# Last steps of the attention part in their own order, softplus moved to the first pairs, twelve residual tiles loaded in one go

## The chip, the cores and the metric

The kernel runs on one core of one Trainium2 chip. The metric is the device time of one execution in microseconds (us); the value compared is the median over several executions. The engines are called as the profile calls them: PE is TensorE, PEld its weight loads, DVE VectorE, ACT ScalarE, POOL GpSimd, and SP the engine that issues nearly all DMAs.

## What is computed

Two transformer layers on 32 sequences of 192 tokens (64 image patches and 128 text tokens), width 256, all in float32. `_layernorm` is the usual normalisation over the last axis.

```python
h = _L0_tok_ref(x, L0_tok_W, L0_tok_b)                       # patches @ W + b
h = concatenate([h, take(weight, x_txt)], axis=1)            # text embeddings
h = h + _L0_attn_ref(_layernorm(h), wq, wk, wv)              # causal softmax attention, one head
h = h + _L0_ffn_ref(_layernorm(h), w_up, w_down)             # ternary weights, rms-normed, gelu, 256-1024-256
h = h + _L1_attn_ref(_layernorm(h), omega, Win, Wl, bl, Wv, bv, Wout)   # a recurrence over the 192 steps
h = h + _L1_ffn_ref(_layernorm(h), routing, experts)         # 8 experts on the first 2 x 256 rows
...
# in _L1_attn_ref:
xi, z = split(x @ Win.T)
log_lam = -8 * softplus(omega) * sigmoid(xi @ Wl.T + bl); lam = exp(log_lam)
v = xi @ Wv.T + bv
h_t = lam_t * (h_prev - 2 v_t (v_t . h_prev) / (v_t . v_t)) + (1 - lam_t) * xi_t
out = (silu(z) * h) @ Wout.T
```

## The kernel before

The program has three parts, each a block that all five engines enter and leave together.

**Part A** (`part_a`, about 0 to 449 us) is the first layer. Work is done in 16 pairs of sequences; a pair is three tiles of 128 tokens. Matrix products are split into a "hi" and a "lo" half (`_hi` made by a copy, `_lo` by a subtraction), which are multiplied separately. The order is written by hand in one list, `order`, that all engines walk: `run` calls `step(g)` for g = -4 to 15, and in a step every entry of the list is done for pair g + offset. The offset is 0 for the feed-forward entries (`up`, `gelu`, `add`, `down`, `ss`, `rscale`, `h2`), 1 for the middle of attention (`pT`, `v`, `pv`, `h1`, `root2`, `scale2`, `x2T`, `x2_split`, `exp_table`) and 2 to 4 for what comes earlier. So in step 14 there is nothing left to do for offsets 2 and up, and in step 15 only pair 15's feed-forward is left. Steps 2 to 11 are a hardware loop. `prepare(g)` holds what is done once, ahead of a step.

The entries that matter here, for pair n:
- `up` k = 0 to 7: PE multiplies by the ternary up weights; `gelu` k: ACT computes gelu, DVE (k 0 to 4) or ACT (5 to 7) makes `gelu_hi`, POOL makes `gelu_lo`; `add` k: DVE adds the squares. In pair 15 alone DVE makes `gelu_lo` for k = 1, 3, 5, 7.
- `down` k = 0, 1, 2: PE multiplies by the down weights; `down.0` waits for each `gelu_lo` in turn. `ss`: PE sums the squares, DVE writes `rms_mean`; `rscale`: POOL's `rms_root`, then DVE's `rms_scale`; `h2`: DVE's final `residual` (L688), which SP stores to DRAM (L285, L287). `up.0` and `up.1` of the next pair wait for it, for they use its PSUM banks.
- `h1`: DVE's `residual` of attention with the statistics of the second norm (L651 to L662); `root2`: POOL's `ln_roots` (L366); `scale2`: DVE's `x_normed` (L681); `x2T`: PE transposes it; `x2_split`: ACT and DVE make `x2T_hi` and `x2T_lo`.
- `turn_win` and `fold` prepare weights of part B: `turn_win` transposes raw_Win on PE (8 instructions, L791), ACT copies it to `Win_rows` (L423), and eight `fold` products of 512 columns (L799) multiply it with raw_Wl. They stand in step 15: `turn_win` and `fold.0` first, one fold after `up.4`, six behind `down.2`.
- The softplus of omega (L494 to L523): `softplus_arg` ahead of step 14, ACT's Exp and Ln at `exp_table` of step 14 with three loads of function tables (L428 to L432), `softplus_one` in `scale2` of pair 15, `softplus_rest` (nine small DVE instructions) ahead of step 15. SP then writes the result to DRAM (L254), and part B reads it as `channel_rows`.

**Part B** (`part_b`, to about 891 us) is the recurrence, in 48 tiles of four time steps, 128 rows of 256 each. SP loads `B_residual` tiles (`load`, L986), 128 KB each, into 12 buffers: four ahead of the loop over i, then tile i + 9 in round i, so that tiles 4 to 7 come in the rounds -5 to -2 and tiles 8 to 11 in the rounds -1 to 2, each just ahead of that round's `B_scan_in` transfer. That transfer (L1033) is four DMAs of 256 KB, 1 MB a round, from one buffer in SBUF to another with the layout that the recurrence needs. ACT may write the staging buffer again (L1206) only when the transfer of two tiles before has landed, and DVE's step of the recurrence (L1241) and POOL's `B_decayed_u` (L1084) wait for it as well. PE alternates between projections (L1350) and the small product of each time step (L1362).

**Part C** is the expert layer and is not touched.

## Time and profile before

| | us |
|---|---|
| median of 3 runs | 974.67 (972.14 to 975.5) |
| the profiled execution's own time | 972.92 |
| its span in the profile | 970.9 |
| PE busy | 933.2 (96%) |
| DVE busy | 791.1 (81%) |
| ACT busy | 591.7 (61%) |
| POOL busy | 544.8 (56%) |

The span is what the rows below lie in; the execution's own time is 2.0 us longer. A busy share says how long instructions of an engine were under way, not that the engine did useful work at its peak. The granted clock of PE is given as a share of full speed: 1.00 is 2.4 GHz and 0.50 is 1.2 GHz.

### The profile page before, as it was taken

Reading aid. Unit: us, or ns where it says so; the run is one execution under the profiler, and the core shown is the slowest. Engines: PE = TensorE matmul, PEld = TensorE weight load, DVE = VectorE, ACT = ScalarE, POOL = GpSimd, SP = SyncE. Lnnn points to the kernel's source line nnn. Section 1 sums busy time; section 2 is a strip of 40 time slices with the busy share of each in tenths; the row PEclk is TensorE's granted clock in tenths of the full one; section 3 lists DMA queues with packets and bytes.
Section 4 is the critical chain, followed back from the end, with each engine's and each line's share of the span. In section 5 each row is a group of like instructions: output and inputs, shape, how many; then the busy total and the mean of one; then the engine's idle time right before and its main releaser. Section 6 shows DMA issues by size and latency. Waiting matters only on the chain. (4 is left out here: it accounts for less than half of the span.)

```text
span 970.9 us, 19833 instructions
## 1 busy us (share of the span) xinstructions
PE 933.2 (96%) x6016; PEld 835.8 (86%) x6016; DVE 791.1 (81%) x2380; ACT 591.7 (61%) x1180; POOL 544.8 (56%) x674
## 2 busy tenths in 40 slices
PE   7899999999999999988999999999999999998998
PEld 6799999999999999865688888888888888887887
DVE  4887777778877777774589999999999988996787
ACT  2266666666666666674667667667667766753442
POOL 4267666666666666444455455445455556552673
PEclk9999999999999999999999999999999999999999
DMA  6001111111111132003899999999999999994220
GB/s 227 24 29 44 39 45 44 43 43 43 43 43 43 43 106 80 17 17 114 109 140 154 153 156 162 146 157 159 158 156 170 180 167 150 148 147 84 99 65 23
DMA packets 63020, 96.35 MB, mean 99 GB/s; under 512 B 12372, under 2 KB 32988, under 8 KB 62300
## 3 DMA queue, kind: packets, MB, share of 16 engines
q1 hardware_dynamic: 61396, 91.19, 50.6%
q0 software_dynamic: 1536, 4.20, 1.4%
q8 instruction: 37, 0.61, 0.3%
q14 instruction: 43, 0.35, 0.2%
q10 hardware_dynamic: 8, 0.00, 0.0%
HBM read 31.90 MB, written 13.11 MB: 46 GB/s over the span
## 5 line engine op out<-in xcount | busy, mean ns | idle before, releaser
L341 POOL TENSOR_TENSOR gelu_lo<-gelu_out,gelu_hi 128x384 fp32r<-128x384 f32 x124 | 146.0, 1206 | 29.0 <-DVE gelu_hi L559 28.5
L1072 POOL TENSOR_TENSOR B_y<-B_scan_in,B_states 128x512 f32<-128x512 f32 x47 | 60.6, 1290 | 79.3 <-ACT B_states L1161 79.3
L765 PE MATMUL psAB<-ternary_down,gelu_hi 128*128 128x256 f32 x384 | 97.0, 291 | 5.8 <-POOL gelu_lo L341 4.9
L698 PE MATMUL psAB<-x2T_hi,ternary_up 128*128 128x384 f32 x256 | 92.7, 362 | 0.8 <-DVE residual L688 0.6
L765 PE MATMUL psAB<-ternary_down,gelu_lo 128*128 128x256 f32 x384 | 93.4, 282 | 0.0
L698 PE MATMUL psAB<-x2T_lo,ternary_up 128*128 128x384 f32 x256 | 86.2, 337 | 0.0
L1350 PE MATMUL psAB<-Win_hi,B_x_hi 128*128 128x512 f32 x192 | 83.4, 434 | 0.0
L765 PEld LDWEIGHTS psAB<-ternary_down,gelu_hi 128*128 128x128 f32 x384 | 72.2, 188 | 10.4 <-POOL gelu_lo L341 8.8
L1084 POOL TENSOR_TENSOR B_decayed_u<-B_scan_in 128x512 f32<-128x512 f32 x48 | 62.2, 1295 | 29.1 <-DMA B_scan_in<-B_stage 24.1
L1257 DVE SCALAR_TENSOR_TENSOR psAB<-B_decayed_u,psAB 128x128 f32<-128x128 f32 x192 | 68.0, 354 | 12.5 <-PE psAB L1362 11.3
L1362 PEld LDWEIGHTS psAB<-B_partial_dots,B_minus_same_batch 128*128 128x128 f32 x384 | 65.3, 190 | 14.3 <-DVE B_partial_dots L1241 4.2
L1350 PE MATMUL psAB<-Win_hi,B_x_lo 128*128 128x512 f32 x192 | 75.5, 393 | 0.0
L1350 PE MATMUL psAB<-Win_lo,B_x_hi 128*128 128x512 f32 x192 | 75.3, 392 | 0.0
L765 PEld LDWEIGHTS psAB<-ternary_down,gelu_lo 128*128 128x128 f32 x384 | 72.6, 189 | 0.0
L1078 POOL TENSOR_TENSOR B_v_scale<-B_half_vv,half_powers 128x1 f32<-128x1 f32 x48 | 26.4, 551 | 78.8 <-ACT B_v_squared L1182 75.7
L410 ACT ACTIVATE gelu_out<-psAB 128x384 f32<-128x384 f32 x128 | 62.6, 490 | 10.3 <-PE psAB L698 10.0
L1241 DVE CUSTOM_DVE_ANT_0 B_products<-B_scan_in,psAB 128x128 f32<-128x128 f32 x192 | 55.1, 287 | 13.4 <-DVE psAB L1257 8.0
L1246 DVE TENSOR_TENSOR psAB<-psAB,B_scan_in 128x128 f32<-128x128 f32 x192 | 57.5, 299 | 6.5
L578 DVE TENSOR_TENSOR gelu_sq_sum<-gelu_sq_sum,gelu_sq 128x384 f32<-128x384 f32 x105 | 61.1, 582 | 1.7
L1362 PE MATMUL psAB<-B_partial_dots,B_minus_same_batch 128*128 128x1 f32 x384 | 54.7, 212 | 3.9 <-DVE B_partial_dots L1241 3.6
L397 ACT ACTIVATE gelu_sq<-gelu_out 128x384 f32<-128x384 f32 x112 | 57.3, 527 | 0.0
L698 PEld LDWEIGHTS psAB<-x2T_hi,ternary_up 128*128 128x128 f32 x256 | 48.0, 188 | 10.6 <-ACT gelu_out L410 8.0
(275 smaller groups left out, 3318.1 us busy)
## 6 DMA issues: line engine op xcount, KB each, us to landing
B_scan_in<-B_stage SPq DMA_DIRECT2D x192, 256.0 KB, 7.0
patches<-in_patches SPq DMA_DIRECT2D x16, 384.0 KB
B_residual<-layer_out SPq DMA_DIRECT2D x48, 128.0 KB, 4.0
out_dram<-B_residual SPq DMA_DIRECT2D x48, 128.0 KB, 3.6
layer_out<-residual SPq DMA_DIRECT2D x32, 128.0 KB, 1.8
raw_Win<-in_experts SPq DMA_DIRECT2D x3, 768.0 KB, 4.3
raw_Wl<-in_experts SPq DMA_DIRECT2D x3, 768.0 KB, 4.2
layer_out<-residual SPq DMA_DIRECT2D x32, 64.0 KB, 1.9
```

The costliest lines, as they stand in the source:

```text
L341: nc.gpsimd.tensor_tensor(act_l[:, k, :], act[:, k % DEEP, :], act_h[:, k, :].bitcast(F32), ALU.subtract).then_inc(s["ffn_lo"], 1)
L397: nc.scalar.activation(out, act[:, k % DEEP, :], ACT.Square).then_inc(s["sq_done"], 1)
L410: nc.scalar.activation(act[:, k % DEEP, :], ps[:, 6 + k % 2, 0:GT], ACT.Gelu).then_inc(s["gelu_done"], 1)
L578: nc.vector.tensor_tensor(sqsum[:], sqsum[:], sq[:, k % DEEP, :], ALU.add).then_inc(s["sqsum_done"], 1)
L698: last = nc.tensor.matmul(out, a, b, start=(n == 0), stop=(n == len(terms) - 1))
L765: last = nc.tensor.matmul(ps[:, 6 + k // 2, (k % 2) * D:(k % 2 + 1) * D], x[:, c, k * P:(k + 1) * P], dn_w[:, c, :], start=(c == 0 and x i ...
L1072: nc.gpsimd.tensor_tensor(y[:, j % 2], ring[:, j % R_RING, :, GATE, :], hs[:, j % 2], ALU.mult).then_inc(s["y"], 1)
L1084: nc.gpsimd.tensor_tensor(lu[:, j % 2], ring[:, j % R_RING, :, LAM, :], ring[:, j % R_RING, :, U, :], ALU.mult).then_inc(s["lu"], 1)
L1246: nc.vector.tensor_tensor(state(j, k), state(j, k), ring[:, j % R_RING, k, DRIVE, :], ALU.subtract).then_inc(s["scan"], 1)
L1257: nc.vector.scalar_tensor_tensor(out=state(i, k), in0=lu[:, i % 2, k, :], scalar=dot[:, t % 2:t % 2 + 1], in1=state(i, k), op0=ALU.mult, o ...
L1350: last = nc.tensor.matmul(out, a, b, start=(not biased and ks[0] == 0 and n == 0), stop=(ks[-1] == DC - 1 and n == len(terms) - 1), skip_g ...
L1362: nc.tensor.matmul(dot[:, t % 2:t % 2 + 1], minus[:], part[:, t % 2:t % 2 + 1], start=True, stop=True).then_inc(s["dot"], 1)
```

## The change

Four things are changed.

1. Step 14 gets an order of its own, `order_late`: `h1` stands behind `gelu.4`, `root2` behind `h1`, `scale2` behind `exp_table`, `x2_split` behind `x2T` and `turn_win` (now with offset 1) behind `x2_split`. In step 15 the folds 0 to 3 stand first, fold 4 behind `up.4` and folds 5 to 7 behind `down.2`. From pair 14 on DVE makes `gelu_lo` for odd k and adds squares with the two-input form that it had for pair 15 alone.
2. Softplus is computed in the first pairs: the vectors are loaded ahead of step -2, `softplus_arg` follows `x_split` of pair 0, Exp and `softplus_one` follow `pT_split` of pair 0, Ln follows `t_split` of pair 1 (with a table load before it and one after, back to Exp), and `softplus_rest` stands ahead of step 12. At `exp_table` of pair 15 nothing is done any more.
3. SP writes `channel_rows` ahead of step 14 instead of step 15.
4. In part B all 12 `B_residual` tiles are loaded ahead of the loop, each with a semaphore of its own (four are cleared first).

```diff
+        order_late = [w for w in order if w[0] not in ("h1", "root2", "scale2", "x2_split")]
+        for what, behind in (("h1", ("gelu", 4)), ("root2", ("h1", 0)), ("scale2", ("exp_table", 0)), ("x2_split", ("x2T", 0)),
+                             ("turn_win", ("x2_split", 0))):
+            order_late.insert(order_late.index(behind) + 1, (what, 0))
...
-        order_last.insert(0, ("turn_win", 0))
-        for m, behind in enumerate((("turn_win", 0), ("up", 4), ("down", 2), ("down", 2), ("down", 2), ("down", 2), ("down", 2), ("down", 2))):
...
+        order_last = [("fold", m) for m in range(4)] + order_last
+        order_last[order_last.index(("up", 4)) + 1:order_last.index(("up", 4)) + 1] = [("fold", 4)]
+        order_last[order_last.index(("down", 2)) + 1:order_last.index(("down", 2)) + 1] = [("fold", m) for m in (5, 6, 7)]
...
-                step(g, g % 2, g // 2, order_last if g == G - 1 else order)
+                step(g, g % 2, g // 2, order_last if g == G - 1 else order_late if g == G - 2 else order)
...
-                if kind == "gelu" and k in lo_pool and not (isinstance(n, int) and n == G - 1 and k in last_lo_vector):
+                if kind == "gelu" and k in lo_pool and not (late(n) and k in late_lo_vector):
...
+                if kind == "pT_split" and isinstance(n, int) and n == 0:
+                    sc.wait_ge(s["c1"], 1)
+                    nc.scalar.activation(soft[:, 1, :], soft[:, 0, :], ACT.Exp, scale=-1.0).then_inc(s["c2"], 1)
+                if kind == "t_split" and isinstance(n, int) and n == 1:
+                    sc.wait_ge(s["c3"], 1)
+                    nc.scalar.activation(soft[:, 3, :], soft[:, 2, :], ACT.Ln).then_inc(s["c4"], 1)
+                    nc.scalar.activation(warm_back[:], ones[:, 0:1], ACT.Exp)
...
-                if g == G - 2:
-                    softplus_arg()
-                if g == G - 1:
+                if g == G - 4:
                     softplus_rest()
...
+            for q in range(8, R_RES):
+                sp.sem_clear(res_in[q])
             for j in range(2):
                 load(j)
...
-            for j in range(2, 4):
+            for j in range(2, R_RES):
                 load(j)
...
-                if has(i + 9):
+                if has(i + 9) and i + 9 >= R_RES:
                     load(i + 9)
```

How the order of instructions moves is best seen in three places. The rows name line, operation, output and inputs; the line numbers of the change are 4 to 9 higher than those of before.

The first is POOL in steps 14 and 15. Before, all eight `gelu_lo` of pair 14 stand ahead of `root2` (L362 to L366):

```order
L341 TENSOR_TENSOR gelu_lo<-gelu_out,gelu_hi 128x384 x8
L362 TENSOR_SCALAR ln_pair<-ln_moments 128x3
L363 TENSOR_SCALAR ln_pair<-ln_moments 128x3
L366 TENSOR_TENSOR ln_roots<-ln_pair,half_powers 128x6
L358 TENSOR_TENSOR rms_root<-rms_mean,half_powers 128x3
L341 TENSOR_TENSOR gelu_lo<-gelu_out,gelu_hi 128x384 x4
```

Now it is:

```order
L350 TENSOR_TENSOR gelu_lo<-gelu_out,gelu_hi 128x384 x3
L371 TENSOR_SCALAR ln_pair<-ln_moments 128x3
L372 TENSOR_SCALAR ln_pair<-ln_moments 128x3
L375 TENSOR_TENSOR ln_roots<-ln_pair,half_powers 128x6
L350 TENSOR_TENSOR gelu_lo<-gelu_out,gelu_hi 128x384
L367 TENSOR_TENSOR rms_root<-rms_mean,half_powers 128x3
```

Four of the eight `gelu_lo` went to DVE; of POOL's own four (k = 0, 2, 4, 6) the last now stands behind the square roots.

The second is PE from `x2T` of pair 15 to `up.0` of pair 15, at the seam of steps 14 and 15. Before, with the end of `down.2` in the first two rows:

```order
L765 MATMUL psAB<-ternary_down,gelu_hi 128x256
L765 MATMUL psAB<-ternary_down,gelu_lo 128x256
L774 MATMUL psAB<-ones,gelu_sq_sum 128x1 x3
L791 MATMUL psAB<-ident,raw_Win 128x128 x8
L799 MATMUL psAB<-raw_Wl,Win_rows 128x512
L698 MATMUL psAB<-x2T_hi,ternary_up 128x384
```

Now, from the last products of `down.1` over `x2T` and `turn_win` to the first of the 16 products of `down.2`:

```order
L771 MATMUL psAB<-ternary_down,gelu_hi 128x256
L771 MATMUL psAB<-ternary_down,gelu_lo 128x256
L715 MATMUL psAB<-ident,x_normed 128x128 x6
L797 MATMUL psAB<-ident,raw_Win 128x128 x8
L771 MATMUL psAB<-ternary_down,gelu_hi 128x256
```

And from the last of those 16 to `up.0`:

```order
L771 MATMUL psAB<-ternary_down,gelu_hi 128x256
L771 MATMUL psAB<-ternary_down,gelu_lo 128x256
L780 MATMUL psAB<-ones,gelu_sq_sum 128x1 x3
L805 MATMUL psAB<-raw_Wl,Win_rows 128x512 x4
L704 MATMUL psAB<-x2T_hi,ternary_up 128x384
```

The transposes went ahead of `down.2`, and four folds instead of one stand between `ss` and `up.0`.

The third is SP at the start of part B. Before (`ISA x37` are semaphores being cleared):

```order
L986 DMA B_residual<-layer_out 128x1x256 x2
L996 ISA x37
L986 DMA B_residual<-layer_out 128x1x256 x4
L1033 DMA B_scan_in<-B_stage 32x4x512 x4
L986 DMA B_residual<-layer_out 128x1x256
L1033 DMA B_scan_in<-B_stage 32x4x512 x4
```

Now, from the load of raw_Wout on:

```order
L1001 DMA B_raw_Wout<-in_WoutT 128x1024
L993 DMA B_residual<-layer_out 128x1x256 x10
L1005 ISA x37
L1042 DMA B_scan_in<-B_stage 32x4x512 x16
L1032 DMA out_dram<-B_residual 32x4x256
```

The first four `B_scan_in` transfers have no tile load between them any more. On DVE, `softplus_rest` now stands between the loop's last instruction and the first CAST of step 12 (L553); there was nothing there before.

## Rows read from the trace of the kernel before

**Rows 1.** Stages of 25 us; columns: core length, busy (count) of each engine, clock, DMA.

```profile
300.00:325.00 25.00, 24.73 (x185) 23.94 (x184) 19.63 (x56) 16.33 (x34) 17.36 (x17) 1.00 0.14 42
```

**Rows 2.** PE's waits, 401 to 449 us: total, times, longest.

```profile
PE psAB L765 <- POOL gelu_lo L341: 1.9, 3, 1.0
PE psAB L709 <- DVE x_normed L681: 1.3, 1, 1.3
PE psAB L841 <- DVE x2T_lo L551: 1.2, 1, 1.2
PE psAB L799 <- ACT Win_rows L423: 0.7, 1, 0.7
```

**Rows 3.** PE, 414 to 449 us: start, duration, what, idle before it and releaser.

```profile
417.96 0.39 PE L765 MATMUL psAB<-ternary_down,gelu_hi 128*128 128x256 f32 x1 [0.95 <-POOL gelu_lo L341]
421.62 0.88 PE L709 MATMUL psAB<-ident,x_normed 128*128 128x128 f32 x6 [1.26 <-DVE x_normed L681]
424.25 0.73 PE L774 MATMUL psAB<-ones,gelu_sq_sum 128*128 128x1 f32 x6
427.55 0.44 PE L698 MATMUL psAB<-x2T_hi,ternary_up 128*128 128x384 f32 x1
443.23 5.31 PE L799 MATMUL psAB<-raw_Wl,Win_rows 128*128 128x512 f32 x12
```

**Rows 4.** DVE and POOL in steps 14 and 15, columns as in rows 3.

```profile
410.43 1.18 DVE L559 CAST gelu_hi<-gelu_out 128x384 fp32r<-128x384 f32 x1
416.03 0.31 DVE L662 BATCH_NORM_AGGREGATE ln_moments<-ln_stats 128x2 f32<-128x6 f32 x3
430.92 0.56 DVE L565 SCALAR_TENSOR_TENSOR gelu_lo<-gelu_out,gelu_hi 128x384 fp32r<-128x384 f32 x1
418.71 1.35 POOL L366 TENSOR_TENSOR ln_roots<-ln_pair,half_powers 128x6 f32<-128x6 f32 x1
```

**Rows 5.** SP's queue, 427 to 460 us: waits, total, times, longest.

```profile
SPq L292 <- DMA layer_out<-residual: 1.4, 1, 1.4
SPq L73 <- PEq L73: 0.5, 1, 0.5
```

**Rows 6.** Step 12, 350 to 370 us: DVE, POOL and PE.

```profile
358.65 0.96 DVE L551 TENSOR_TENSOR v_lo<-psAB,v_hi 128x768 fp32r<-128x768 f32 x1 [0.61 <-ACT v_hi L386]
361.22 5.53 POOL L341 TENSOR_TENSOR gelu_lo<-gelu_out,gelu_hi 128x384 fp32r<-128x384 f32 x4 [1.15 <-DVE gelu_hi L559]
368.74 0.39 PE L765 MATMUL psAB<-ternary_down,gelu_hi 128*128 128x256 f32 x1 [0.26 <-POOL gelu_lo L341]
```

**Rows 7.** DVE, softplus_rest ahead of step 15: its first instruction and the next after it.

```profile
427.81 0.16 DVE L508 TENSOR_SCALAR softplus<-softplus 128x4 f32<-128x4 f32 x1
429.22 0.36 DVE L559 CAST gelu_hi<-gelu_out 128x384 fp32r<-128x384 f32 x1
```

**Rows 8.** ACT: after t_split of pair 1, and a table load of step 14.

```profile
49.23 0.81 ACT L464 ACTIVATE x2T_hi<-psAB 128x768 fp32r<-128x768 f32 x1 [5.51 <-PE psAB L709]
418.37 1.28 ACT L430 ACT_TABLE_LOAD   x1
```

**Rows 9.** Landing of the first scan transfer, then of residual tile 8: time from issue.

```profile
L1033 SPq DMA_DIRECT2D B_scan_in<-B_stage x4: 605/608/658, 465.8 to 467.8; - x4
DMA to landing us min/median/max: 4.3/6.4/8.2
L986 SPq DMA_DIRECT2D B_residual<-layer_out x1: 623/623/623, 468.4 to 468.4; - x1
DMA to landing us min/median/max: 8.3/8.3/8.3
```

**Rows 10.** ACT and PE at the second scan transfer's landing.

```profile
485.37 0.69 ACT L1206 ACTIVATE B_stage<-psAB,B_v_scale 128x512 f32<-128x512 f32 x1 [2.59 <-DMA B_scan_in<-B_stage]
487.21 0.47 PE L1350 MATMUL psAB<-Wl_Win_hi,B_x_hi 128*128 128x512 f32 x1 [1.11 <-ACT psAB L1143]
```

**Rows 11.** PE's clock, 488 to 491 us; columns as in rows 1.

```profile
488.00:491.00 3.00, 3.00 (x9) 0.50 1.05 137
```

More of the change, by code:

```diff
@@ L112, in part_a @@
         sq = sb("gelu_sq", [P, DEEP, GT])
-        warm, warm_gelu = sb("exp_table_warm", [P, 1]), sb("gelu_table_warm", [P, 1])
+        warm, warm_gelu, warm_back = sb("exp_table_warm", [P, 1]), sb("gelu_table_warm", [P, 1]), sb("exp_table_back", [P, 1])
         sqsum = sb("gelu_sq_sum", [P, GT])
@@ L218, in part_a, with late @@
         lo_pool = [k for k in range(FC) if k not in lo_vector]
-        last_lo_vector = (1, 3, 5, 7)
+        LATE = G - 2
+        late_lo_vector = (1, 3, 5, 7)
+        def late(n):
+            return isinstance(n, int) and n >= LATE
         def wait_lo(eng, n, k):
@@ L227, in wait_lo @@
                 return
-            if isinstance(n, int) and n == G - 1:
-                if k in last_lo_vector:
-                    eng.wait_ge(s["ffn_lo_v"], last_lo_vector.index(k) + 1)
+            if late(n):
+                if k in late_lo_vector:
+                    eng.wait_ge(s["ffn_lo_v"], 4 * (n - LATE) + late_lo_vector.index(k) + 1)
                 else:
-                    eng.wait_ge(s["ffn_lo"], FC * n + k // 2 + 1)
+                    eng.wait_ge(s["ffn_lo"], FC * LATE + 4 * (n - LATE) + k // 2 + 1)
             elif k in lo_vector:
@@ L249, in prepare @@
                     sp.dma_start(ids[:, 0, :], io["ids"][0]).then_inc(ids_in[0], 16)
-                if g == G - 4:
+                if g == -2:
                     sp.dma_start(vec[:], io["vectors"]).then_inc(s["vec_in"], 16)
-                if g == G - 1:
+                if g == G - 2:
                     sp.wait_ge(s["c8"], 1)
@@ L424, in piece @@
                                              ps[:, (4, 2)[half_nat], :], ACT.Copy).then_inc(s["nat_ready"], 1)
-                if kind == "exp_table" and isinstance(n, int) and n == G - 1:
-                    sc.wait_ge(s["c1"], 1)
-                    nc.scalar.activation(soft[:, 1, :], soft[:, 0, :], ACT.Exp, scale=-1.0).then_inc(s["c2"], 1)
-                    sc.wait_ge(s["c3"], 1)
-                    nc.scalar.activation(soft[:, 3, :], soft[:, 2, :], ACT.Ln).then_inc(s["c4"], 1)
-                    wait(sc, s["gelu_warmed"], G)
-                    nc.scalar.activation(warm_gelu[:], ones[:, 0:1], ACT.Gelu)
-                elif kind == "exp_table":
+                if kind == "exp_table" and not (isinstance(n, int) and n == G - 1):
                     wait(sc, s["warmed"], n)
@@ L525, in prepare @@
             def prepare(g):
-                if g == G - 2:
-                    softplus_arg()
-                if g == G - 1:
+                if g == G - 4:
                     softplus_rest()
@@ L559, in piece @@
                     nc.vector.tensor_copy(act_h[:, k, :], act[:, k % DEEP, :]).then_inc(s["ffn_hi"], 1)
-                if kind == "gelu" and isinstance(n, int) and n == G - 1 and k in last_lo_vector:
+                if kind == "gelu" and late(n) and k in late_lo_vector:
                     if k in hi_scalar:
@@ L567, in piece @@
                                                    op1=ALU.subtract).then_inc(s["ffn_lo_v"], 1)
-                if kind == "add" and isinstance(n, int) and n == G - 1:
+                if kind == "add" and late(n):
                     v.wait_ge(s["sq_done"], FC * n + k + 1)
@@ L583, in piece @@
                         chunk_lo(2)
+                        softplus_arg()
                 if kind == "t_split":
@@ L594, in piece @@
                     nc.vector.reciprocal(rinv[:], rowsum[:]).then_inc(s["rinv_done"], 1)
+                    if isinstance(n, int) and n == 0:
+                        softplus_one()
                 if kind == "qk_split" and isinstance(n, int) and n == 0:
@@ L669, in piece @@
                 if kind == "scale2":
-                    if isinstance(n, int) and n == G - 1:
-                        softplus_one()
                     v.wait_ge(s["ln2_roots"], n + 1)
@@ L934, in part_b @@
             E.s[name] = E.stack.enter_context(nc.semaphore("C_" + name))
+        res_in += [ctx.enter_context(nc.semaphore("B_res_in%d" % q)) for q in range(8, R_RES)]
         def wait_res_in(eng, j):
-            eng.wait_ge(res_in[j % 8], 16 * (j // 8 + 1))
+            eng.wait_ge(res_in[j % R_RES], 16 * (j // R_RES + 1))
         def wait_arrived(eng, j):
@@ L1002, in _ @@
                         wait_stored(sp, j)
-                    sp.dma_start(E.acc[:, q, :], io["out"][q, 0:P, :]).then_inc(res_in[(TT + q) % 8], 16)
+                    sp.dma_start(E.acc[:, q, :], io["out"][q, 0:P, :]).then_inc(res_in[(TT + q) % R_RES], 16)
                 if i == TT:
```

8 lines of the change are left out of this document (2 added, 6 removed).

## The prediction

> **What bounds the kernel now.** I read the stages first. In the middle of part A, PE is busy 24.73 of 25 us at full clock, DVE 19.63, ACT 16.33, POOL 17.36 [rows 1]: PE sets the pace, and an edit is worth only what it does to PE's idle time. I then read PE's waits from step 14 to the end of part A, in total and in order of time. They are few: 1.9 us for POOL's `gelu_lo`, 1.3 for `x_normed`, 1.2 for `x2T_lo`, 0.7 for `Win_rows` [rows 2]. The wait for `x2T_lo` is at the end of step 13, whose order isn't changed. PE ends part A with six folds, 5.31 us, so 0.885 us a fold [rows 3]. SP had by then waited 1.4 us for the last stores and stood another 0.5 us for PE [rows 5]: PE closes part A, with a slack of only 0.5 us over the path of h2 and store. Last I read the start of part B. Transfers are the limit there: the 16 DMA engines are full (share 1.05) while PE runs at half clock [rows 11], ACT waited 2.59 us for the second scan transfer, and PE 1.11 us for ACT's next piece [rows 10].
>
> **Softplus in the first pairs.** The new DVE pieces are one small instruction each; the length of the nine of `softplus_rest` is 429.22 - 427.81 = 1.41 us, 0.16 each [rows 7]. Both fall next to waits of DVE for ACT; cost 0. ACT gets Ln, Exp and two table loads behind `t_split` of pair 1: 2 x 1.28 plus 2 x 0.2 = 3.0 us, in a wait of 5.51 us for PE [rows 8]; cost 0, and were the cover gone, 3.0. The Trainium skill, "ScalarE: Activation LUTs", section "What ACT_TABLE_LOAD costs", gives about 2.66 us for each switch, since a drain comes on top of the load; two switches would be 5.3 us and with the activations just over the cover. The trace does not bear this out: the load at 418.37 is 1.28 us. The vectors' load is one small DMA behind the patches on SP, and its landing has 14 us until DVE wants it; 0.
>
> Taken away in step 14 are three table loads and two activations of ACT, ahead of `x2T_hi`, and 1.41 us of DVE ahead of step 15. Neither was on PE's path: `x_normed` was late by POOL, not by ACT [rows 2, 4], and the CAST at 429.22 [rows 7] needs a gelu of the product that started at 427.55 [rows 3], so it could hardly come sooner. Gain 0.
>
> `softplus_rest` now stands ahead of step 12, in the full pipeline. What is queued behind it on DVE is the whole step. DVE has one cover there, 0.61 us of waiting ahead of `v_lo`; behind it everything is late by 1.41 - 0.61 = 0.8 us. Then comes `x_normed`, then the CAST of gelu 2, for which POOL already waits (1.15 us), and POOL's six remaining `gelu_lo` run nearly back to back into `down.0`, for which PE already waits 0.26 us [rows 6]. So the 0.8 us reach PE; a little contention more, and I take **+0.9**. Bounds: 0, if POOL catches up; 1.4, if nothing is covered.
>
> **Step 14.** Next follow `h1`. Its aggregate ended at 416.34, and POOL's roots at 420.06, for they stood behind `gelu_lo` 7 [rows 4]. Now three adds stand behind it, two `gelu_lo` of 0.56 ahead of it, and CASTs that took 1.18 beside a running POOL come nearer to 0.36 [rows 4, 7]; I put the aggregate at 415.7. POOL's roots take 1.35 us [rows 4] and the two small instructions ahead some 0.45, so roots at 417.5. But POOL's `gelu_lo` 6 now stands behind them and, at 1.2 us (mid-way in the lengths of rows 6: 5.53 for four is 1.38), ends at 418.7. `down.0` needs it before its seventh chunk. Before, PE resumed at 417.96 with 18 products left, was done at 421.62 - 1.26 = 420.36 (0.13 each) and began `x2T` at 421.62 [rows 3]. Now it resumes at about 418.7 with 20 left, and reaches `x2T` at 418.7 + 2.6 = 421.3 without waiting for `x_normed` (ready at about 419.7). **-0.3**: one wait is traded for another, and PE stands idle some 2.6 us in one piece.
>
> `turn_win` ahead of `down.2` adds 0.95 us to everything behind it (eight transposes; the six of `x2T` took 0.88 with their overlap [rows 3]). From `ss` to `up.0` it took 427.55 - 424.25 = 3.30 us [rows 3], set by the chain ss, rms, `h2`, with transposes, a 0.7 us wait and one fold in it. Now: 0.59 for `ss` (0.73 less its overlap) and four folds, 4 x 0.885 = 3.54, are 4.13; the chain of 3.3 is covered, and **+0.83** remains. So `up.0` of pair 15 comes at -0.3 + 0.95 + 0.83 = +1.5. Step 15 is otherwise alike (a fold behind `up.4` in both), so `h2` and the last store come 1.5 later. The three folds that left the end shorten PE's tail by 2.65 us, but the store path binds at once: only its slack of 0.5 is gained [rows 5]. **+1.0** for the end of part A. Bounds: -0.6, if `gelu_lo` 6 comes in time and `x2T` can start with `x_normed` at 419.7; +1.5, if nothing of the slack counts. The row for `channel_rows` goes out a step sooner: 0.
>
> **Twelve tiles at once.** The first scan transfer's last part landed at 467.8 + 8.2 = 476.0, tile 8 at 468.4 + 8.3 = 476.7 [rows 9]: what is issued later lands behind. Tile 8 stood ahead of the second transfer for 0.7 us; by bytes (1.125 MB in the 9.3 us to 485.3) its share is 1.0. I take **-0.9** for the second transfer. ACT's 2.59 us of waiting and PE's 1.11 shrink by it [rows 10]; it is the nearest thing in the program to a full gain. The tiles themselves are loaded in SP's first 12 us, when nothing needs the queue; SP is free long before the first scan transfer at 465.8 [rows 9]. Tiles 9 to 11 stood ahead of transfers with slack. Bounds: 0 to -1.1. The four clears cost 0.2 us on SP ahead of tile 0, hidden behind PE's merges.
>
> **The clock.** PE stood idle 0.5 and 1.11 us [rows 10] shortly before its clock was at 0.50, 1.2 GHz, for 3 us [rows 11]; that costs half, 1.5 us. With 0.9 less of idle time the fall may not come: -1.5. In turn, the new idle piece of 2.6 us in step 14, and one of about 2 us at the seam of A and B, may each bring one: +1.5 each. I count -1.5 and half of +1.5: **-0.75**. The Trainium skill, "TensorE: Matmul & The Clock Gate", section "HAM oscillation", says that gaps in PE's work bring the half clock back and that each is paid again; by that rule both new gaps are suspects, which is the slower rival below.
>
> **Sum.** 0.9 + 1.0 - 0.9 - 0.75 = +0.25. From the profiled execution's 972.92 that is 973.2; the median of the runs shown is 1.75 above this execution, so I forecast 974.67 + 0.25 = **974.9**, no change. A measurement of this kernel can't tell less than 0.3% (2.9 us) from no change.
>
> **Rivals.**
> - *Faster: the gains come and the costs hide.* `softplus_rest` is absorbed (0), step 14 pays (-0.6), the second transfer gives -1.1 and the clock -1.5: -3.2, 971.5. For it: the waits it would fill are real. Against it: POOL's queue order and PE's waits for it in step 12. It ends beyond 0.3% only if all four come. Chance 0.18.
> - *Slower: the clock falls at a new gap.* The piece of 2.6 us in step 14 and the seam each cost 1.5, and the fall at 488 stays: 0.9 + 1.0 - 0.9 + 3.0 = +4.0, 978.7. For it: 1.6 us of idle time went before the fall at 488. Against it: 1.2 us in one piece at 402 was followed by none [rows 2]. It decides if both come. Chance 0.14.
> - *The tile loads never mattered*: no transfer gain and no clock gain, 0.9 + 1.0 = +1.9, 976.6. It speaks for it that the four parts of a transfer spread over all engines; against it the landing times. Chance 0.15.
> - *Step 14 alone pays*, -1.6 against the sum: 973.3. Chance 0.10.
>
> **How the numbers follow.** The likeliest case has 0.43; its own range is 973.5 to 976. It, the third and the fourth lie within 0.3%, 0.68 together; faster 0.18, slower 0.14. The range leaves out half of each outer case: 971.2 to 978.0.
>
> **What would show it.** In the changed profile: PE's wait at the start of `down.0` of step 12 near 1.1 instead of 0.26; in step 14 one wait of about 2.5 for POOL's `gelu_lo` and none for `x_normed` or `Win_rows`; `up.0` of pair 15 later by 1.5 behind step 13; PE idle some 2 us ahead of part B and SP no longer waiting for PE; tile loads all issued within 12 us, ACT's wait for the second scan transfer below 2, and the clock's row at 488 to 491 near 1.00. Wrong would be: `gelu_lo` 6 ready in time, a clock below 1 in the stage 415 to 420 or 449 to 455, or scan transfers that land as late as before.

## The result, and the profile after

In 20 executions of each kernel the changed one took 975.87 us in the median (974.10 to 978.94), the one before 973.57 (970.94 to 975.50). The ratio is 1.0026, 95% interval 1.0017 to 1.0034: 2.5 us slower (1.7 to 3.3), at the edge of what can be told from no change. The forecast was +0.25 us, 974.9. (The ratios and intervals here are the record's estimates; they are not the quotient of the two medians, though mostly near it.)

The profiled execution of the changed kernel took 978.94 us, the slowest of the 20, with a span of 977.0 and a mean granted clock of 0.991; the profiled one before had 0.996. So this trace shows 6.1 us more where the medians differ by 2.3, and its clock has to be read first. "A fall" below is a stretch in which the granted clock goes from 1.00 to 0.50 and back. Windows of the changed kernel, columns as in [rows 1]:

```profile
10.00:15.00 5.00, 4.02 (x20) 3.96 (x21) 1.21 (x3) 0.00 (x0) 0.00 (x0) 0.68 1.00 410
300.00:325.00 25.00, 24.75 (x185) 23.95 (x185) 19.61 (x57) 16.33 (x34) 17.34 (x17) 1.00 0.14 42
350.00:375.00 25.00, 23.67 (x174) 22.57 (x173) 22.10 (x64) 16.32 (x34) 15.95 (x17) 1.00 0.41 149
405.00:410.00 5.00, 3.89 (x19) 3.69 (x20) 3.53 (x10) 3.32 (x6) 1.38 (x2) 0.78 0.21 56
425.00:430.00 5.00, 5.00 (x33) 5.00 (x32) 2.68 (x5) 1.79 (x3) 0.00 (x0) 0.68 0.00 0
455.00:460.00 5.00, 4.26 (x7) 1.90 (x8) 2.33 (x7) 4.29 (x6) 2.48 (x9) 0.66 0.46 150
490.00:495.00 5.00, 3.92 (x21) 2.97 (x19) 4.17 (x16) 2.60 (x7) 2.04 (x3) 1.00 1.06 136
905.00:910.00 5.00, 4.07 (x21) 3.72 (x21) 1.72 (x3) 2.39 (x3) 4.13 (x2) 0.66 0.47 145
```

The reader is to see a steady state like before (24.75 against [rows 1]), a step 12 in which PE is busy 1.1 us less than that, and five windows with a clock (third column from the end) below 1: at 10 to 15, 405 to 410, 425 to 430, 455 to 460 and 905 to 910, each with a stretch at 1.2 GHz. The fall of [rows 11] is gone, its window reads 1.00. The kernel before had two, that of [rows 11] and one in part C. Next PE's waits in steps 14 and 15 and at the seam, in total and then in order of time, as [rows 2, 3]:

```profile
PE psAB L771 <- POOL gelu_lo L350: 3.0, 2, 2.4
PE psAB L1348 <- PEq L73: 2.5, 1, 2.5
PE psAB L847 <- DVE x2T_lo L557: 1.2, 1, 1.2
```

```profile
405.46 0.73 PE L847 MATMUL psAB<-ident,probs 128*128 128x128 f32 x5 [1.21 <-DVE x2T_lo L557]
426.55 1.48 PE L715 MATMUL psAB<-ident,x_normed 128*128 128x128 f32 x6
434.53 0.74 PE L704 MATMUL psAB<-x2T_hi,ternary_up 128*128 128x384 f32 x1
455.74 2.04 PE L1348 MATMUL psAB<-raw_Wv,Win_rows 128*128 128x512 f32 x2 [2.52 <-PEq L73]
```

The waits for `x_normed` and `Win_rows` are gone, as forecast, and one of 2.45 us for POOL's `gelu_lo` stands in their place. Why, POOL's rows show: the roots stand ahead of `gelu_lo` 6, as [rows 4] had them behind.

```profile
420.03 0.37 POOL L371 TENSOR_SCALAR ln_pair<-ln_moments 128x3 f32<-128x3 f32 x1 [1.77 <-DVE ln_moments L671]
420.94 1.35 POOL L375 TENSOR_TENSOR ln_roots<-ln_pair,half_powers 128x6 f32<-128x6 f32 x1
422.26 1.00 POOL L350 TENSOR_TENSOR gelu_lo<-gelu_out,gelu_hi 128x384 fp32r<-128x384 f32 x1
```

Step 12 by PE's waits and the DVE and POOL rows that answer to [rows 6, 7]:

```profile
361.83 0.36 PE L704 MATMUL psAB<-v_hi,probT_hi 128*128 128x256 f32 x1 [0.44 <-DVE v_lo L557]
367.66 0.44 PE L704 MATMUL psAB<-xT_hi,qk_hi 128*128 128x384 f32 x1 [0.89 <-DVE xT_lo L557]
```

```profile
355.62 0.16 DVE L516 TENSOR_SCALAR softplus<-softplus 128x4 f32<-128x4 f32 x1
356.94 0.17 DVE L531 TENSOR_SCALAR channel_vectors<-softplus 128x4 f32<-128x4 f32 x1
360.73 0.95 DVE L557 TENSOR_TENSOR v_lo<-psAB,v_hi 128x768 fp32r<-128x768 f32 x1
361.60 1.76 DVE L645 TENSOR_SCALAR x_normed<-embedded,ln_moments,ln_rstd 128x256 f32<-128x256 f32 x3
364.02 1.16 DVE L565 CAST gelu_hi<-gelu_out 128x384 fp32r<-128x384 f32 x1
366.66 0.94 DVE L557 TENSOR_TENSOR xT_lo<-psAB,xT_hi 128x768 fp32r<-128x768 f32 x1
```

```profile
360.86 2.03 POOL L350 TENSOR_TENSOR gelu_lo<-gelu_out,gelu_hi 128x384 fp32r<-128x384 f32 x2
363.71 1.25 POOL L350 TENSOR_TENSOR gelu_lo<-gelu_out,gelu_hi 128x384 fp32r<-128x384 f32 x1 [0.83 <-DVE gelu_hi L565]
```

Last, the second scan transfer, as [rows 9, 10]: its landing from issue, then who waited, and SP's ten tile loads after the first two.

```profile
DMA to landing us min/median/max: 7.6/9.6/11.4
```

```profile
493.36 0.69 ACT L1215 ACTIVATE B_stage<-psAB,B_v_scale 128x512 f32<-128x512 f32 x1 [2.26 <-DMA B_scan_in<-B_stage]
495.20 0.47 PE L1359 MATMUL psAB<-Wl_Win_hi,B_x_hi 128*128 128x512 f32 x1 [1.10 <-ACT psAB L1152]
458.41 6.62 SPq L993 DMA_DIRECT2D B_residual<-layer_out  x10
```

ACT still waits 2.26 us and PE 1.10, where it was 2.59 and 1.11.

**The clock from one execution to the next.** Each execution comes with its mean granted clock, and these stand in steps: in the traces 1.000 goes with no fall of the clock, 0.998 with one, 0.996 with two, 0.995 with three, 0.992 with four and 0.991 with five, some 0.0018 a fall. In one set of 27 executions of the kernel before the three fastest (970.41 to 970.63 us) have 0.998 and the slowest (975.95) has 0.991. A line with one slope for all 249 executions of this study and a level for each kernel gives 0.63 us for each 0.001 of clock and leaves 0.7 us of scatter: most of the spread of some 5 us within a kernel goes with its clock. The mean clock over all executions of each kernel, beside the times of the experiments:

| kernel | median us | before, run beside it | ratio, 95% interval | mean clock |
|---|---|---|---|---|
| changed | 975.87 | 973.57 | 1.0026 [1.0017, 1.0034] | 0.9944 |
| tiles_only | 973.47 | 973.00 | 1.0006 [0.9993, 1.0018] | 0.9951 |
| softplus_only | 975.70 | 973.00 | 1.0027 [1.0016, 1.0039] | 0.9948 |
| order_only | 974.45 | 973.00 | 1.0028 [1.0013, 1.0042] | 0.9939 |
| rest_at_15 | 976.50 | 973.00 | 1.0039 [1.0024, 1.0055] | 0.9921 |
| first_pairs_only | 973.86 | 973.51 | 1.0004 [0.9989, 1.0018] | 0.9956 |
| late_plain | 973.03 | 973.51 | 1.0002 [0.9988, 1.0015] | 0.9941 |
| late_gelu6 | 972.61 | 973.51 | 1.0003 [0.9992, 1.0014] | 0.9934 |
| held_clock | 970.28 | 973.51 | 0.9973 [0.9962, 0.9983] | 0.9979 |
| softplus_held | 971.60 | 973.34 | 0.9988 [0.9976, 1.0001] | 0.9982 |
| order_held | 970.85 | 973.34 | 0.9977 [0.9965, 0.9990] | 0.9983 |
| after_held | 972.37 | 973.34 | 0.9996 [0.9984, 1.0008] | 0.9982 |
| gelu6_held | 969.53 | 973.34 | 0.9963 [0.9951, 0.9976] | 0.9984 |

The kernel before had a mean clock of 0.9953, 0.9956 and 0.9952 in the three sets in which it ran beside the experiments; for its 20 executions beside the changed kernel none is on record. The ratio of order_only is above that of its medians, 1.0015, and rests on 9 executions; for late_gelu6 the medians give 0.9991.

### The profile page after: what moved, and what is told of

The parts are those of the page before. It is cut to its first block and busy times, and to the rows that moved or that the text cites. A ratio compares the mean times of both kernels' runs of the same rounds, so it can differ in the third digit from the quotient of the medians.

```text
span 977.0 us, 19836 instructions
## 1 busy us (share of the span) xinstructions
PE 936.4 (96%) x6016; PEld 839.3 (86%) x6016; DVE 792.9 (81%) x2384; ACT 590.4 (60%) x1179; POOL 538.9 (55%) x670
## 5 line engine op out<-in xcount | busy, mean ns | idle before, releaser
L350 POOL TENSOR_TENSOR gelu_lo<-gelu_out,gelu_hi 128x384 fp32r<-128x384 f32 x120 | 141.0, 1202 | 33.0 <-DVE gelu_hi L565 33.0
L584 DVE TENSOR_TENSOR gelu_sq_sum<-gelu_sq_sum,gelu_sq 128x384 f32<-128x384 f32 x98 | 56.3, 575 | 1.5
```

The lines of the kernel that those rows point to most:

```text
L350: nc.gpsimd.tensor_tensor(act_l[:, k, :], act[:, k % DEEP, :], act_h[:, k, :].bitcast(F32), ALU.subtract).then_inc(s["ffn_lo"], 1)
```

## The experiments

The first four take the change apart, the next four look for the mechanism in step 14 and for the clock, the last four repeat the parts with the clock held up.

**tiles_only**: of the change only the twelve loads, their semaphores and clears.

```diff
-            for j in range(2, 4):
+            for j in range(2, R_RES):
                 load(j)
```

> Only the twelve tile loads, with their semaphores, are taken over into the kernel before. Theory 1 (my forecast): tile 8 no longer stands ahead of the second scan transfer, ScalarE's wait for it falls from 2.59 us to about 1.7, TensorE's wait of 1.11 us for ScalarE's next piece shrinks and the half clock at 488 to 491 goes: 0.9 to 2.4 us faster than before. Theory 2 (the changed kernel's trace, where the 1.11 us wait stood unchanged at 1.10): only about 0.3 us comes of the transfer, and the half clock comes or stays away from one execution to the next whatever the loads: within 0.5 us of before.

Measured: no change, 1.0006 (0.9993 to 1.0018). Landing of the second transfer from issue, ACT's wait for it, PE's behind that, and the clock at 490:

```profile
DMA to landing us min/median/max: 7.9/10.0/11.9
487.42 0.69 ACT L1209 ACTIVATE B_stage<-psAB,B_v_scale 128x512 f32<-128x512 f32 x1 [2.43 <-DMA B_scan_in<-B_stage]
489.26 0.47 PE L1353 MATMUL psAB<-Wl_Win_hi,B_x_hi 128*128 128x512 f32 x1 [1.10 <-ACT psAB L1146]
490.00:495.00 5.00, 5.00 (x21) 4.14 (x20) 3.35 (x12) 2.60 (x7) 1.55 (x4) 0.66 1.03 137
```

The last part lands 11.9 us after issue; the kernel before had 485.3 - 473.5 = 11.8. Tile 8 stood ahead of it, but its absence gives nothing: theory 2. (In the changed kernel it is 11.4, with PE's wait the same.) The half clock at 490 is there without tile 8 as well. The 1.10 us could not shrink with an earlier landing, they only move: what PE does just before them (487.77) waits for the landing too, by way of DVE, and what ends them is the third of three ACT instructions from the landing on (487.42, 488.01, 488.53).

**softplus_only**: of the change only the softplus edits (item 2 and 3 of the change).

```diff
-                if g == G - 1:
+                if g == G - 4:
                     softplus_rest()
```

> Only the move of the softplus pieces is taken over. Theory 1 (the step 12 term): the nine small DVE instructions ahead of step 12 reach TensorE by way of DVE's v_lo and xT_lo, for 1.3 us (forecast: 0.9, by way of POOL's gelu_lo), and steps 14 and 15 gain nothing: 0.9 to 1.5 us slower than before, step 12 at 26.4 us from tok to tok instead of 25.1. Theory 2 (the pieces in the first pairs cost too, as the changed kernel's trace had its first pairs 1.2 us later): 2.3 to 2.7 slower. Theory 3 (steps 14 and 15 give back what step 12 takes): within 0.5.

Measured: +2.6 us (1.6 to 3.8). Theory 1 missed. The size is theory 2's, but not its reason, as first_pairs_only shows below. PE's waits in step 12 are the changed kernel's, 0.4 for `v_lo` and 0.9 for `xT_lo`. The wait at the end of step 13, 1.21 us as before [rows 2], is now followed by a fall, which the trace of the kernel before does not have:

```profile
404.39 0.74 PE L838 MATMUL psAB<-ident,probs 128*128 128x128 f32 x5 [1.21 <-DVE x2T_lo L548]
405.00:410.00 5.00, 4.35 (x22) 4.23 (x21) 2.67 (x7) 2.25 (x6) 1.28 (x2) 0.66 0.37 81
```

**order_only**: of the change only the orders of steps 14 and 15 and DVE's half of `gelu_lo`.

```diff
-                step(g, g % 2, g // 2, order_last if g == G - 1 else order)
+                step(g, g % 2, g // 2, order_last if g == G - 1 else order_late if g == G - 2 else order)
```

> Only the orders of steps 14 and 15, with DVE's half of the gelu_lo in step 14, are taken over. Theory 1 (my forecast's term): the end of part A comes 1.0 us later. Theory 2 (the changed kernel's trace: a wait of 2.45 us for POOL's gelu_lo, after which the clock fell, and a wait of 2.5 us at the seam): 2 to 4 us slower than before, with the half clock seen behind either gap. Theory 3: the gaps hide in the store path and step 14 pays: 0.5 faster to 0.5 slower.

Measured: +2.7 us (1.3 to 4.1; the medians differ by 1.5), theory 2 in the main, for the clock falls behind one of the two gaps alone and stays whole behind the seam. The end of part A comes 2.55 us later (451.39 against 448.84), and the clock falls behind the long wait for `gelu_lo`; the wait of 1.21 us at 402 is followed by none here, and the fall at 490 is gone although nothing is changed in part B.

```profile
402.71 0.74 PE L850 MATMUL psAB<-ident,probs 128*128 128x128 f32 x5 [1.21 <-DVE x2T_lo L560]
405.00:410.00 5.00, 5.00 (x36) 4.76 (x35) 3.46 (x8) 3.50 (x8) 1.02 (x1) 1.00 0.28 80
419.01 0.45 PE L774 MATMUL psAB<-ternary_down,gelu_hi 128*128 128x256 f32 x1 [2.45 <-POOL gelu_lo L350]
420.00:425.00 5.00, 5.00 (x35) 5.00 (x35) 3.02 (x7) 3.14 (x6) 0.00 (x0) 0.74 0.01 2
451.39 1.10 PE L1348 MATMUL psAB<-raw_Wv,Win_rows 128*128 128x512 f32 x2 [2.52 <-PEq L73]
490.00:495.00 5.00, 5.00 (x29) 4.21 (x28) 4.75 (x19) 3.54 (x8) 2.36 (x4) 1.00 1.07 150
```

**rest_at_15**: the changed kernel with `softplus_rest` ahead of step 15 again, and SP's write of `channel_rows` with it.

```diff
-                if g == G - 4:
+                if g == G - 1:
                     softplus_rest()
```

> The changed kernel with softplus_rest ahead of step 15 again, and the row's store with it; the other softplus pieces stay in the first pairs. Theory 1 (the term is step 12's): 1.0 to 1.4 us faster than the changed kernel, so about 1.2 slower than before, and step 12 is 25.1 us long again. Theory 2 (the cost only moves: ahead of step 15 the 1.41 us stand in front of DVE's half of the gelu_lo and of the h2 path): as slow as the changed kernel, 2.5 slower than before.

Measured: 1.0039, in 7 executions, not faster than the changed kernel: theory 1 missed. Step 12 is whole again (PE busy 24.57 in the 25 us from 350, 23.67 in the changed kernel), but this kernel has the lowest mean clock of all, 0.9921, and its trace has falls at 420 to 425, at the seam, in the middle of part B and in part C. Its time says nothing sure of the term; the traces of the kernels that have `softplus_rest` in step 12 do (see *Step 12* below).

**first_pairs_only**: the kernel before with the softplus pieces in the first pairs, `softplus_rest` ahead of step 15 as before.

```diff
...
+                if kind == "t_split" and isinstance(n, int) and n == 1:
+                    sc.wait_ge(s["c3"], 1)
+                    nc.scalar.activation(soft[:, 3, :], soft[:, 2, :], ACT.Ln).then_inc(s["c4"], 1)
+                    nc.scalar.activation(warm_back[:], ones[:, 0:1], ACT.Exp)
...
```

> The kernel before with the softplus argument, its Exp and Ln and the first add in the first pairs, and the nine instructions of softplus_rest ahead of step 15 as before. Theory 1 (all of the softplus edit's cost is softplus_rest in step 12): within 0.4 us of before, step 12 at 25.1 us. Theory 2 (the first pairs cost by themselves, as the softplus_only kernel was 2.6 us slower with only 1.3 us of waits in step 12): 0.8 to 1.3 us slower than before.

Measured: +0.04% (-0.11 to +0.18), theory 1, though the upper end of the interval reaches theory 2. The trace is closer: after the first pairs, the work is 0.1 us later than before, and 0.3 later at the end of step 13. The table loads hide, and with softplus_only the cost is left to step 12 and the clock.

**late_plain**: the new order of step 14 alone, with `turn_win` and the folds in step 15 as before. Against the changed kernel `order_late` differs in this:

```diff
-        for what, behind in (("h1", ("gelu", 4)), ("root2", ("h1", 0)), ("scale2", ("exp_table", 0)), ("x2_split", ("x2T", 0)),
-                             ("turn_win", ("x2_split", 0))):
+        for what, behind in (("h1", ("gelu", 4)), ("root2", ("h1", 0)), ("scale2", ("exp_table", 0)), ("x2_split", ("x2T", 0))):
```

> Step 14 alone: h1, the roots and scale2 early and half of the gelu_lo on DVE as in the changed kernel, turn_win and the folds where they were in the kernel before. Theory 1 (the wait of 2.45 us for POOL's gelu_lo brings the half clock behind it each time): that wait is seen, x2T of pair 15 comes 1.4 us later than before, the end of part A as much, the seam wait is near 0.3 us again, 0.7 to 1.7 us slower than before. Theory 2 (turn_win ahead of down.2 and the four folds are what costs): within 0.4 us of before.

Measured: no change (1.0002). The wait of 2.45 us is there with a fall behind it, `x2T` starts at 424.34 (one more fall, at 405, lies ahead of it), and the seam wait is 0.33. By time theory 2 holds, but the interval (0.9988 to 1.0015) reaches theory 1: this profiled execution, with four falls, has the mechanism of theory 1 in it. What order_only has beyond late_plain is `turn_win` ahead of `down.2` and the folds, with the 2.5 us gap at the seam.

**late_gelu6**: late_plain with the roots one place later.

```diff
-        for what, behind in (("h1", ("gelu", 4)), ("root2", ("h1", 0)), ("scale2", ("exp_table", 0)), ("x2_split", ("x2T", 0))):
+        for what, behind in (("h1", ("gelu", 4)), ("root2", ("gelu", 6)), ("scale2", ("exp_table", 0)), ("x2_split", ("x2T", 0))):
```

> As late_plain, but POOL's roots stand behind its gelu_lo 6. Theory 1 (the order on POOL makes the long wait): gelu_lo 6 ends near 416.2 and costs PE nothing, the roots end near 418.3, x2T of pair 15 starts near 420.9, 0.7 us earlier than before, without a half clock at 420 to 425; 0.5 to 1.0 us faster than before. Theory 2 (what is left of the waits, 1.2 us for DVE's gelu_lo 7 and 0.5 us for x_normed, still brings the half clock): as slow as before or up to 1 us slower.

Measured in the trace: nearly as theory 1 says. The long wait is two short ones, `x2T` starts at 421.09 (before 421.62), part B at 448.30 (before 448.84), and the clock is whole at 420 to 425. But PE was 0.30 us ahead already at the end of step 13 (402.50 against 402.80), so steps 14 and 15 gain only 0.24. In time: 1.0003, no gain; its mean clock is 0.9934, lower than before.

```profile
416.50 0.38 PE L776 MATMUL psAB<-ternary_down,gelu_hi 128*128 128x256 f32 x1 [0.85 <-DVE gelu_lo L576]
418.59 0.39 PE L776 MATMUL psAB<-ternary_down,gelu_hi 128*128 128x256 f32 x1 [1.34 <-DVE gelu_lo L576]
421.09 0.87 PE L720 MATMUL psAB<-ident,x_normed 128*128 128x128 f32 x6
475.00:480.00 5.00, 3.06 (x10) 2.26 (x10) 2.85 (x11) 2.70 (x5) 2.49 (x5) 0.79 1.08 149
```

**held_clock**: the kernel before with idle transposes in nine places (eight more at startup among them), into a bank that nobody reads then. One of them:

```diff
+                if kind == "pT" and isinstance(n, int) and n == G - 1:
+                    pe.wait_ge(s["max_done"], G)
+                    for _ in range(7):
+                        nc.tensor.transpose(ps[:, 2, 0:P], ident[:], ident[:])
```

> The kernel before with idle TensorE transposes of the identity queued ahead of eight of its waits (startup 8 more, pT of pair 15 7, up.0 of step 14 3, the eighth chunk of down.0 in step 14 5, x2T of pair 15 7, the first dots of part B 11 and 2, project l of step 1 of part B 6, part C's first expert 5), each a little shorter than the wait. It does no useful work more. Theory 1 (the half clock follows on idle pieces and costs 3 us in the mean execution): mean clock 0.998 or more, 1.0 to 2.5 us faster than before, and executions that spread less than 4 us. Theory 2 (the clock falls whatever stands in the waits): clock 0.995 as before and the time the same or up to 1 us more.

Measured: 0.9973, 2.6 us faster, executions from 968.84 to 972.45, mean clock 0.9979: theory 1. DVE's steps of the work start at most 0.2 us earlier up to 478; the wait at 402 is only shorter, and the window at 490 is whole.

```profile
402.65 0.74 PE L854 MATMUL psAB<-ident,probs 128*128 128x128 f32 x5 [0.38 <-DVE x2T_lo L551]
490.00:495.00 5.00, 5.00 (x33) 4.46 (x31) 4.13 (x16) 2.84 (x7) 1.96 (x3) 1.00 1.09 151
```

**softplus_held, order_held, after_held, gelu6_held**: four of the kernels above with such transposes. After_held and order_held have two in places of their own:

```diff
+                            if isinstance(n, int) and n == G - 2 and c in {6: 15}:
+                                turns_in(2, {6: 15}[c])
...
+            for _ in range(15):
+                nc.tensor.transpose(ps[:, 2, 0:P], ident[:], ident[:])
```

> The softplus_only kernel with the idle transposes of held_clock. Theory 1 (the edit's cost is the waits of 0.44 and 0.89 us in step 12, and what else softplus_only lost was the clock): 1.3 us slower than held_clock, so about 0.13% faster than before. Theory 2 (it costs 2 us or more of work somewhere): 0.05% faster than before or slower.

> The order_only kernel with the transposes of after_held. Theory 1 (the order of step 14 gains 0.1 and turn_win and folds cost 1.3 us, the rest of order_only's loss is the clock): 1.0 to 1.3 us slower than held_clock, 0.13 to 0.17% faster than before, the clock at 1.00 from 420 to 460. Theory 2 (the wait of 2.45 us itself costs): as slow as before or slower.

> The changed kernel with idle transposes of the identity in TensorE's waits, sized a little under each: startup 8 more, pT of pair 15 7, up.0 of step 14 3, the seventh chunk of down.0 in step 14 15 (the wait of 2.45 us for POOL's gelu_lo), the end of part A 15 (the wait of 2.5 us at the seam), part B's first dots 11 and 1, project l of step 1 of part B 6, part C 5. Theory 1 (part of the changed kernel's loss is the half clock behind its new gaps, part is work): mean clock 0.997 or 0.998, 2 to 2.5 us faster than the changed kernel (within 0.5 us of before), and 2 to 3 us slower than the kernel before with such transposes, 0.27% faster than before. Theory 2 (all of the change's loss is the clock): as fast as that one, 0.2 to 0.3% faster than before.

> The late_gelu6 kernel (step 14 with the roots behind gelu_lo 6, turn_win and folds as before, no other edit) with such transposes: ahead of the sixth and eighth chunk of down.0 4 and 7, otherwise as held_clock without those of x2T. Theory 1 (late_gelu6's gain of 0.5 us in the trace was lost to the clock): 0.3 to 0.9 us faster than held_clock, 0.30 to 0.37% faster than before. Theory 2 (the gain was chance): as held_clock.

Measured: softplus_held, after_held and gelu6_held near their theory 1; order_held is 0.4 us slower than held_clock where 1.0 to 1.3 was expected. Against held_clock (0.9973) the differences of the ratios are +0.15% for softplus_held (1.5 us), +0.04% for order_held (0.4), +0.23% for after_held (2.2) and -0.10% for gelu6_held (-1.0). Each ratio is known to some 0.12%, and held_clock's is from another set, so a difference is known to about 1.6 us: only after_held's is clear of that.

The traces are finer, if the time is taken from one place that both kernels have. From `pT` of pair 15, at the end of step 13, to the first product of part B it is 448.84 - 402.80 = 46.04 us before (first two rows) and 449.66 - 402.51 = 47.15 in order_held (the other rows), 1.11 more; after_held has 452.41 - 405.23 = 47.18. From `pT` to `x2T` it is 18.82 before and 18.77 in order_held.

```profile
402.80 0.74 PE L841 MATMUL psAB<-ident,probs 128*128 128x128 f32 x5 [1.21 <-DVE x2T_lo L551]
448.84 7.11 PE L1339 MATMUL psAB<-raw_Wv,Win_rows 128*128 128x512 f32 x16 [0.30 <-PEq L73]
402.51 0.74 PE L861 MATMUL psAB<-ident,probs 128*128 128x128 f32 x5 [0.39 <-DVE x2T_lo L560]
418.81 0.38 PE L785 MATMUL psAB<-ternary_down,gelu_hi 128*128 128x256 f32 x1 [0.81 <-POOL gelu_lo L350]
420.00:425.00 5.00, 5.00 (x47) 5.00 (x45) 3.49 (x7) 3.60 (x7) 0.00 (x0) 1.00 0.00 2
421.28 0.82 PE L718 MATMUL psAB<-ident,x_normed 128*128 128x128 f32 x6
428.43 0.74 PE L707 MATMUL psAB<-x2T_hi,ternary_up 128*128 128x384 f32 x1
449.66 0.67 PE L1361 MATMUL psAB<-raw_Wv,Win_rows 128*128 128x512 f32 x1 [0.89 <-PEq L73]
```

The same stretch gives the price of a fall. Order_only has one fall in it and takes 451.39 - 402.71 = 48.68 us, 1.53 more than order_held; the changed kernel has two and takes 455.74 - 405.46 = 50.28, 3.13 more. A fall costs 1.5 to 1.6 us here.

Gelu6_held is the fastest kernel of the study, 0.37% (0.24 to 0.49) faster than before, and held_clock (0.27%) is most of it.

## Why the prediction was right, and where it was not

No change was forecast, and the ratio lies within 0.3%. But +0.25 us was forecast and 2.5 measured (1.7 to 3.3), since of the four terms two did not hold, and both missed to the same side. That the call stands is owed to its width more than to its mechanism: the likeliest case had 973.5 to 976, and the rival *the tile loads never mattered*, at +1.9, is nearer to what was measured.

| term | forecast | measured | from |
|---|---|---|---|
| softplus in the first pairs | 0 | 0 | first_pairs_only, 1.0004; 0.1 in its trace |
| `softplus_rest` ahead of step 12 | +0.9 | +1.3 | PE's waits 0.44 + 0.89 |
| order of steps 14 and 15, to the end of part A | +1.0 | +1.1 | order_held, 47.15 - 46.04 |
| second scan transfer | -0.9 | 0 | tiles_only, 11.9 us to landing against 11.8 |
| clock | -0.75 | about +0.9 | mean clock 0.9944 against 0.9954 |
| sum | +0.25 | +3.3 | measured +2.5 (1.7 to 3.3) |

The clock's term is an estimate: 1.55 us for a fall and 0.0018 of mean clock for one make 0.9 us for each 0.001, and the changed kernel has 0.0010 less than before (0.9954 is the mean of the other three sets), about half a fall in each execution. By the line within kernels it would be 0.6. The sum lies at the upper end of what was measured, 0.8 us above its middle, and that rest is not accounted for. Without the clock, after_held stands 2.2 us above held_clock, and the terms of work give 1.3 + 1.1 + 0 = 2.4.

Not all that idle transposes gain is the clock: held_clock's 0.0023 is worth 2.0 us by this price, or 1.4 by the line, where 2.6 were measured. In its trace some 0.7 us of gain come between 478 and 488, ahead of the place of the fall, about half of it from the second scan transfer (19.0 us from the first issue to the last landing, 19.5 before; 19.2 to 19.3 in the other four kernels with transposes). Why that transfer is quicker there stays open.

**Softplus in the first pairs.** This term was right. I argued against a drain behind each table load from the length of one load, which does not show it. The rows behind it do: the load at 418.37 ends at 419.65 and the next activation begins at 419.67 in the kernel before, and in the changed one the two loads and two activations last from 44.91 to 47.93, the 3.0 us of the forecast.

**Step 12.** The term was under-sized and its path was another. Between DVE's `residual` of pair 11 and that of pair 12 the traces of all four kernels with `softplus_rest` there (changed, softplus_only and both with transposes) have 1.29 to 1.32 us more than before. I took `v_lo` to be 0.8 late; it came 0.7 late (360.73, less 1.38 for the step's later start, against 358.65), and that alone stopped PE for 0.44. What followed did not go by POOL's `gelu_lo` into `down.0`, where PE no longer waits at all, but by `x_normed` and `xT_lo`, for DVE's instructions now ran beside POOL's: `x_normed` took 1.76 us instead of 1.35, the CAST at 364.02 took 1.16 instead of 0.35 beside a `gelu_lo` that had begun at 363.71, the next CAST 1.17, and `xT_lo` came 1.9 late, although DVE's wait of 0.73 us ahead of it, a second cover that I had not counted, was used up as well. The Trainium skill, "SBUF — State Buffer", section "Who interferes with whom", says that DVE and GpSimd share one pair of ports and that one waits for the other whole; the CAST agrees with it, and so do POOL's six `gelu_lo` of [rows 6], 1.24 us each beside short CASTs instead of 1.00 alone: there POOL was the one to wait. That DVE's late start changed which of the two waits is the reading of these rows; no run tried it by itself.

**Step 14.** The places were right: the aggregate at 415.56 in order_only (415.7 forecast), the roots done at 417.99 (417.5), `gelu_lo` 6 done at 418.96 (418.7), one wait of 2.45 (about 2.5). The gain of 0.3 at `x2T` was not there. `x2T` starts 0.34 earlier in order_held than before, but 0.29 of that PE had at the end of step 13 already; taken from there, the new order gains 0.05. Taken from the same place, `up.0` of pair 15 comes 1.2 later (+1.5) and the end of the part 1.1 (+1.0). So the forecast of the end came out partly by luck, with errors that cancel: `x2T` gained nothing, `turn_win` and the folds cost less, and of SP's slack of 0.5 us, which I took off, next to nothing was gained (1.2 at `up.0` is 1.1 at the end). A fold was priced at 5.31 / 6 = 0.885, a busy time that holds the tail of the last product; four folds took 428.43 - 425.31 = 3.12, 0.78 each, and the transposes of `turn_win` 0.8 instead of 0.95. In the profiled execution of the changed kernel `up.0` was 4.3 later behind step 13, since two falls, at 408 and 425, lay ahead of it.

**The tiles.** The step that failed is "what is issued later lands behind", as I drew from it that what is not issued gives back its time. Between the first issue and the last landing of the second transfer lie 19.5 us before (465.8 to 485.3), 19.7 in tiles_only (467.7 to 487.4) and 19.5 in the changed kernel (473.8 to 493.3). The two megabytes take that long with tile 8 between them and without; in all traces it is 19.0 to 19.7. The rival *the tile loads never mattered* was right in this term. What sets the rate of these transfers stays open.

**The clock.** I tied the fall at 488 to the idle time of ACT's wait and let the tiles remove it. They don't. It is missing near 490 where the whole new order is in (order_only, rest_at_15, the changed kernel), and in late_plain and late_gelu6 it comes one wait earlier, behind the 1.95 us for the first dots (in late_gelu6 a clock of 0.79 at 475 to 480). Why it is missing is not settled. For the slower rival I weighed "1.2 us in one piece at 402 was followed by none" as evidence against; in the changed kernel, softplus_only, tiles_only and late_plain the same 1.21 us are followed by a fall, in before, order_only, rest_at_15, first_pairs_only and late_gelu6 not. So an idle piece of that size is a risk, and one trace can't say which. The rival was right that the clock can fall at both new gaps, as it does in the profiled execution and in rest_at_15, and wrong that the old fall stays; in order_only the seam has none. The profiled execution is the slowest, with five falls; the mean of the 20, 0.9944, is about three. The Trainium skill, "TensorE: Matmul & The Clock Gate", section "What's actually happening", says that what the gate looks at runs freely, whatever the kernel does; the same wait with and without a fall behind it agrees with that. That the same gap meets another phase in each execution was not tried by itself.

**What would show it.** Right: no wait for `x_normed` and `Win_rows`, one of 2.5 for `gelu_lo`, 2.52 us of idle PE ahead of part B, the loads out within 9.1 us (455.9 to 465.0), a clock of 1.00 at 488, though with another cause than I gave. Wrong: 1.1 us at `down.0` of step 12 (none), `up.0` later by 1.5 (4.3 here, 1.2 at full clock), SP no longer waiting for PE (0.2 against 0.5), ACT's wait below 2 (2.26). Of the signs against me two came: the clock below 1 behind a new gap, and a second transfer that lands nearly as late as before (11.4 against 11.8).

## What to carry to other kernels

Where PE is near full and the clock still falls in a few waits, two kernels can be told apart only with the clock in view: list the mean clock of every execution beside its time, and test a part of a change with PE's waits filled by idle work. Times alone did not resolve the parts here: the bare kernels gave 2.7 + 2.6 + 0.6 against 2.5 for the whole, and those with transposes 0.4 + 1.5 against 2.2, each known only to 1 us or more. The stretch between two places that both kernels have in their traces did: 1.3 in step 12, 1.1 in steps 14 and 15, and 1.5 to 1.6 for a fall, the same within 0.1 in each kernel that has it. A wait is not worth its length: filling PE's waits with nothing useful gained 2.6 us, more than any new order. And before a transfer's slot is counted as gained, compare the time from first issue to last landing with and without the load that is to go.
